# Two conditioned layers in one kernel: constants sent first, five betas on VectorE, two centrings on ScalarE, a bank for VectorE's scratch, new orders

## The reference

```python
h = _noise_encoding(t, E)                 # sin and cos of 5000 t * freqs, E = 128
h = jax.nn.silu(h @ W1 + b1)              # 512 wide
h = h @ W2 + b2
scale = (h @ Wsc + bsc)[:, None, :]
shift = (h @ Wsh + bsh)[:, None, :]
out = jax.nn.silu(scale * _layer_norm(x, gamma, beta) + shift)
out = out @ W_in + b_in
out = jax.nn.silu(scale * _layer_norm(out, gamma, beta) + shift)
out = out @ W_out + b_out
return out + x
```

## Time and profile before

| | us |
|---|---|
| median of 3 runs (82.25 to 82.94) | 82.47 |
| span of the profiled execution, first to last instruction | 80.7 |
| median less span | 1.77 |
| TensorE, matmuls busy | 75.0 |
| VectorE busy | 61.3 |
| ScalarE busy | 55.8 |
| GpSimd busy | 53.3 |

### The profile page before, as it was taken

One profiled execution on the slowest core, in us unless ns is written; L12 is line 12 of the kernel. 1 busy time (PEld: TensorE's weight loads), 2 busy tenths in 40 slices (PEclk: granted clock), 3 DMA queues, 4 the chain that ended last, 5 costly groups with the idle time before them and its releaser, 6 DMA issues.

```text
span 80.7 us, 1314 instructions
## 1 busy us (share of the span) xinstructions
PE 75.0 (93%) x293; PEld 37.2 (46%) x293; DVE 61.3 (76%) x181; ACT 55.8 (69%) x174; POOL 53.3 (66%) x63
## 2 busy tenths in 40 slices
PE   4999899999989999999999899999999899999950
PEld 1367547468633444444453443444454344445420
DVE  1085797879899979999879868886194697989560
ACT  4202410999939998977999997799936998967000
POOL 4000283999999999999999999999999303020000
PEclk9999999999999999999999999999999999999999
DMA  1799999999500000201130033030307200030835
GB/s 8 279 446 398 426 384 400 406 410 404 238 8 4 0 0 0 103 27 64 70 127 3 0 130 132 6 134 0 130 4 282 108 0 0 0 129 1 325 141 184
DMA packets 4903, 11.92 MB, mean 148 GB/s; under 512 B 672, under 2 KB 928, under 8 KB 4768
## 3 DMA queue, kind: packets, MB, share of 16 engines
q1 hardware_dynamic: 4752, 11.33, 36.7%
q10 hardware_dynamic: 144, 0.52, 1.6%
HBM read 7.65 MB, written 4.19 MB: 147 GB/s over the span
## 4 chain that ended last, share of the span: by engine, by line
POOL 41%; PE 27%; issue 25%; DVE 2%; POOLq 0%; ACT 0%; ACTq 0%
POOL act L326 16%; POOL act L331 11%; PE acc L978 11%; POOL act L320 7%; PE acc L849 6%; POOL rstd L304 5%; PE acc L954 5%; PE acc L989 2%; POOL rstd L314 1%; PE acc L852 1%; PE acc L999 1%; DVE o_sb L716 1%; PE stat_m L1007 1%; PE stat L898 0%; DVE spread L621 0%
## 5 line engine op out<-in xcount | busy, mean ns | idle before, releaser
L426 ACT ACTIVATE act<-act,cond 128x256 f32<-128x256 f32 x64 | 35.9, 594 | 5.6 <-POOL act L331 3.6
L978 PE MATMUL acc<-act,wout_sb 128*128 128x512 f32 x60 | 27.5, 600 | 0.0
L954 PE MATMUL acc<-act,win_sb 128*128 128x512 f32 x56 | 26.9, 608 | 0.5 <-ACT act L426 0.2
L331 POOL TENSOR_TENSOR act<-act,beta_sb 128x512 f32<-128x512 f32 x13 | 16.5, 1281 | 0.7
L326 POOL TENSOR_TENSOR act<-act,gamma_sb 128x512 f32<-128x512 f32 x13 | 16.6, 1284 | 0.3
L978 PEld LDWEIGHTS acc<-act,wout_sb 128*128 128x128 f32 x60 | 10.9, 189 | 12.4 <-issue 9.0
L446 ACT ACTIVATE squares<-acc,shift 128x256 bf16<-128x256 f32 x32 | 14.7, 464 | 2.1 <-PE acc L954 1.3
L704 DVE SCALAR_TENSOR_TENSOR act<-acc,shift,gamma_sb 128x256 f32<-128x256 f32 x32 | 14.3, 476 | 1.4 <-ACT squares L446 1.3
L954 PEld LDWEIGHTS acc<-act,win_sb 128*128 128x128 f32 x56 | 9.8, 190 | 10.5 <-issue 7.5
L711 DVE SCALAR_TENSOR_TENSOR act<-act,rstd,beta_ps 128x512 f32<-128x512 f32 x16 | 11.6, 742 | 3.4 <-issue 2.5
L716 DVE SCALAR_TENSOR_TENSOR o_sb<-acc,const_sb,x_sb 128x512 f32<-128x512 f32 (+1 forms) x17 | 11.9, 713 | 2.4 <-PE acc L978 2.3
(11 more groups left out here) (74 smaller groups left out, 53.7 us busy)
## 6 DMA issues: line engine op xcount, KB each, us to landing
out_dram<-o_sb SPq DMA_DIRECT2D x15, 256.0 KB, 2.0
x_sb<-x_dram SPq DMA_DIRECT2D x7, 512.0 KB, 12.8
w_sb<-w_dram SPq DMA_DIRECT2D x1, 1024.0 KB, 6.2
wss_sb<-wss_dram SPq DMA_DIRECT2D x1, 768.0 KB, 8.5
x_sb<-x_dram ACTq DMA_DIRECT2D x1, 512.0 KB, 3.9
w_sb<-w_dram SPq DMA_DIRECT2D x1, 256.0 KB, 4.1
gamma_sb<-gamma_dram SPq DMA_DIRECT2D x1, 256.0 KB, 6.4
wss_sb<-wss_dram SPq DMA_DIRECT2D x1, 256.0 KB, 8.7
```

What stands on the lines that cost most here:

```text
L331: nc.gpsimd.tensor_tensor(act1[:, p, :, b], act1[:, p, :, b], beta_sb[:], ALU.add).then_inc(z1_pool, 1)
L426: return nc.scalar.activation(buf[:, c, b], buf[:, c, b], ACT.Silu, bias=cond[:, 1, c, i:i + 1], scale=cond[:, 0, c, i:i + 1], **kw)
L954: mm = nc.tensor.matmul(y_slot(p, c)[:].rearrange("p b s -> p (b s)"), win_sb[:, k, c * P:(c + 1) * P], act1[:, p, k].rearrange("p b s -> ...
L978: mm = nc.tensor.matmul(bank_of(("O", p, c, 0, BP))[:].rearrange("p b s -> p (b s)"), wout_sb[:, k, c * P:(c + 1) * P], act2[:, p, k].rear ...
```

## The change

It has six parts. Line numbers in this section's rows are those of each file.

1. x[0] is issued by SyncE behind const, no longer by ScalarE; x[1] is loaded in two halves; x[2] stands ahead of W_in; the last three are x[6], x[7], x[5]. x is stored by item and then half, so that an item's 512 columns lie together.
2. `add_beta` on VectorE takes over GpSimd's `weigh_beta` for (2,1), (4,1), (4,0), (5,0) and (7,1).
3. `centre1` on ScalarE takes over GpSimd's `centre1` for (4,1) and (5,0); their rstd is multiplied in by `add_beta`.
4. All inputs of a statistics matmul stand in one tile, `stat_in`, one row for each matmul (`STATS`), and all powers in `POWERS`; VectorE's scratch moves to the bank `stat_m`; the mean of b_in uses a column of `beta_ps`.
5. `encoding` computes the turns from the constants, no longer from its first result. Products with zeros: 15 instead of 29 and 6 halves.
6. All orders are new. TensorE has 20 statistics matmuls, 16 of them behind the first product (before 15).

```diff
             sp.dma_start(const_sb[:], consts).then_inc(const_in, 16)
+            sp.dma_start(x_sb[:, 0], x[0]).then_inc(x_in[0, 0], 16)
...
-            act.dma_start(x_sb[:, 0], x[0]).then_inc(x_in[0], 16)
             nc.scalar.preload_act_table_set("silu_and_others")
...
-        x_sb = sb("x_sb", [P, NP, C, BP, S])
+        x_sb = sb("x_sb", [P, NP, BP, C, S])
...
+SHIFTED_DVE = ((2, 1), (4, 1), (4, 0), (5, 0), (7, 1))
+CENTRED_ACT = ((4, 1), (5, 0))
...
+            def add_beta(p, b):
+                dve.wait_ge(beta_ps_ready, 1)
+                dve.wait_ge(scaled_pool, count(SCALED_POOL, (p, b)))
+                if (p, b) in CENTRED_ACT:
+                    await_rstd(dve, "1", p)
+                    nc.vector.scalar_tensor_tensor(act1[:, p, :, b], act1[:, p, :, b], rstd_of("1", p, b), beta_ps[:],
+                                                   ALU.mult, ALU.add).then_inc(z1_shifted, 1)
+                else:
+                    nc.vector.tensor_tensor(act1[:, p, :, b], act1[:, p, :, b], beta_ps[:], ALU.add).then_inc(z1_shifted, 1)
...
+            def centre1(p, b):
+                i = BP * p + b
+                act.wait_ge(negm1_ready, count(NEGATED, GROUP_OF[p]))
+                nc.scalar.activation(act1[:, p, :, b], x_sb[:, p, b], ACT.Identity, bias=neg_m1[:, i:i + 1]).then_inc(centred_act, 1)
...
+            def dev_ps(n):
+                return stat_m[:, DEV_COL + 4 * n:DEV_COL + 4 * n + width(n)]
...
+            def stat_bank_free(i):
+
+                for kind, n in STATS[i - 1] if i else ():
+                    if kind == "mean1":
+                        pe.wait_ge(negm1_ready, count(NEGATED, n))
+                        if not summed_by_act(n):
+                            pe.wait_ge(dev_ready, count(DEVIATIONS, n))
...
             pe.wait_ge(zeros_set, 1)
-            warm(N_WARM)
+            warm(5)
```

More of the change, by code:

```diff
@@ L93 @@
 LEASED = ACCUMULATORS - 1
+SUMMED_BY_DVE = tuple(p for p in range(NP) if p not in SUMMED_BY_ACT)
+STAT_OF = {column: i for i, columns in enumerate(STATS) for column in columns}
+POWER_OF = {member: i for i, members in enumerate(POWERS) for member in members}
 def count(order, *items):
@@ L258, in bank_of, with await_x @@
+        def await_x(engine, p, b=None):
+            for i in range(BP) if p in BY_BATCH and b is None else (b,) if p in BY_BATCH else (0,):
+                engine.wait_ge(x_in[p, i], 16)
         def bank_of(product):
@@ L740, in _ @@
-            weigh_rowsums(0)
+            bn_stats1(1, 0)
+            bn_stats1(1, 1)
+            aggregate1(1, 1)
+            aggregate1(1, 0)
+            add_b2()
+            deviation(1)
+            weigh_gamma(0, 0, 0, 1)
+            weigh_gamma(0, 0, 1, 1)
+            negate_mean(1)
+            spread1(1, 1)
+            spread1(1, 0)
+            weigh_gamma(1, 0, 0, 2)
+            weigh_beta(0, 0, 1, 1)
+            weigh_beta(0, 0, 0, 1)
+            add_b_cond()
+            stats1_variance(1)
@@ L743, in _ @@
             mean_shift2(0)
-            stats1(4)
-            stats1_deviation(3)
-            weigh_gamma(2, 0)
+            bn_stats1(4, 0)
+            weigh_beta(2, 0, 0, 2)
+            weigh_rowsum0(1)
+            deviation(3)
+            negate_mean(3)
+            weigh_rowsum1(1)
+            spread1(3, 0)
+            weight2(0, 0, 0)
+            spread1(3, 1)
+            weight2(0, 0, 1)
+            mean_shift2(1)
+            add_beta(2, 1)
             stats1_variance(3)
-            weigh_rowsums(1)
+            bn_stats1(5, 1)
@@ L781, in _ @@
-            finish(1, 0)
-            normalise2(2, 0)
-            weigh_rowsums(4)
-            normalise2(2, 1)
+            aggregate1(7, 0)
+            weight2(2, 0, 1)
+            bn_stats1(7, 1)
+            weigh_rowsum0(3)
+            aggregate1(6, 0)
+            weigh_rowsum1(3)
+            add_beta(4, 1)
+            aggregate1(7, 1)
+            bn_stats1(6, 1)
+            aggregate1(6, 1)
+            mean_shift2(3)
+            variance2(2)
+            weight2(2, 1, 0)
+            weight2(2, 1, 1)
@@ L785, in _ @@
+            negate_mean(5)
+            add_beta(4, 0)
+            deviation(5)
+            finish(0, 1, 0, 2)
+            copy_deviation(5)
+            add_beta(5, 0)
+            square_deviation(5)
+            weigh_rowsum0(4)
+            weigh_rowsum1(4)
+            spread1_pairs(5)
+            finish(1, 0, 0, 2)
             weight2(3, 0, 0)
-            weight2(3, 1, 1)
-            stats1_deviation(5)
-            weight2(3, 1, 0)
             weight2(3, 0, 1)
             mean_shift2(4)
+            stats1_variance(5)
@@ L815, in _ @@
+            weight2(5, 1, 0)
+            finish(2, 1, 0, 2)
+            normalise2(4, 0)
+            weight2(5, 0, 0)
+            weight2(5, 1, 1)
+            weight2(5, 0, 1)
+            weigh_rowsum0(6)
+            weigh_rowsum1(6)
+            add_beta(7, 1)
+            finish(3, 1, 0, 2)
+            normalise2(4, 1)
+            variance2(5)
+            finish(3, 0, 0, 2)
             mean_shift2(6)
-            variance2(5)
-            finish(4, 0)
+            weigh_rowsum0(7)
@@ L830, in _ @@
+            weight2(7, 0, 1)
             weight2(7, 0, 0)
[L831 removed]
             variance2(7)
[L833 removed]
+            finish(4, 1, 0, 2)
+            normalise2(7, 1)
+            finish(4, 0, 0, 2)
+            normalise2(6, 1)
+            finish(5, 0, 0, 2)
+            finish(7, 1, 1, 1)
             normalise2(7, 0)
[L835 to L838 removed]
+            finish(5, 1, 0, 2)
```

927 lines of the change are left out of this document (452 added, 475 removed), and 15 rows, old and new, of tables (PRODUCTS, STATS).

## The result

The changed kernel is slower. Its median is 83.72 us, the kernel before took 82.36 beside it: ratio 1.013, 95% interval 1.007 to 1.020. Measured again it was 84.76 against 82.36, ratio 1.032 (1.023 to 1.040). Its own times spread from 82.7 to 85.8 over the two measurements, those of the kernel before from 82.0 to 82.9; the spread belongs to the change, as the experiments show. Seven of its eight executions took longer than any of the kernel before; the eighth took 82.73. Forecast were 81.9, with 80.8 to 83.4 as range: the 83.72 lie outside, on the side that had a chance of 0.17. The profiled execution took 83.94 us with a span of 82.1, before 80.7.

A forecast was written before the change was run, and what follows sets the result against it. It took the chain of waits as mostly GpSimd's (41%), then TensorE's (27%). Start 15.05 + products 55.0 + statistics 16 x 0.22 + waits 3.7 = 77.25 against 77.85, minus 0.6, giving 81.9 us; range 80.8 to 83.4.

The forecast's parts named there:

- The bytes ahead of beta are the same, so beta lands at 13.0.: Loads at the start: beta's landing stays at 4.39 + 8.6 = 13.0 us, as before.
- The two more issues on SyncE's queue: Start: issues for x[0] and x[1]'s halves, some 0.45 us each, hidden; with an idle queue they would cost 0.9.
- A slow clock: Rival, slower: fewer warming products leave the first layer products at 1.2 GHz, plus 1.3 us, 83.2; chance 0.09.
- From 13.0 to the first Silu: Start: after beta, 0.25 to see it, betas and add_b_cond to 14.3, Silu 0.60; first product's input at 14.95.
- the 1.0 us at the start: Start: the first product begins at 15.05 instead of 16.05 us, minus 1.0.
- x[3] late: Rival, slower: VectorE waits for x[3] at bn_stats of (3,1), from 16.6 us, becoming the bound; 82.9 or 83.6; chance 0.15.
- VectorE takes five betas, GpSimd loses them: VectorE pays 0.66 us per beta, covered by idle time and the earlier start; GpSimd's last beta ends at 58.0, not 62.5.
- ScalarE's centrings: ScalarE centres (4,1) and (5,0) between 30 and 38 us: 0.60 each, 1.2 in all, hidden in 1.4 idle.
- TensorE's waits: Between first and last product, waits at statistics and at products waiting for ScalarE total 3.7 us, against 3.5 before.
- waits go: Rival, faster: VectorE's small instructions cost 0.1 us less in the separate bank, about 1 us of waits goes, 80.9; chance 0.14.

The follow-up runs named there:

- f_gamma_act: Changed kernel with the old products with zeros (29 and 6 halves) and gamma issued by ScalarE at the start, x[0] staying on SyncE's queue: 81.57 us, ratio 0.994.
- b_few_warm: Kernel before with only the changed kernel's products with zeros (15, no halves): 84.65 us.
- a_same: The changed kernel measured again without an edit: 84.76 us, ratio 1.032 to the kernel before.
- e_start: Changed kernel with x[0] from ScalarE's queue, the old products with zeros but fewer at two places, and another VectorE order at the start: 81.53 us, ratio 0.991.
- a_warm: Changed kernel with the products with zeros as before, 29 and 6 halves instead of 15: 83.51 us.
- c_x0_act_warm: Changed kernel with two parts undone, x[0] from ScalarE's queue and the old products with zeros: 81.61 us, ratio 0.9925.
- d_bank_back: Changed kernel with x[0] from ScalarE's queue, the old products with zeros, and VectorE's scratch back in the statistics' bank: 82.29 us, ratio 1.003.

## Why the prediction was wrong, step by step

*The bytes ahead of beta are the same, so beta lands at 13.0.* This step failed. It took the bytes ahead for the only thing that sets a landing, and the trace of before couldn't show otherwise, as it had two queues in use. All in one queue cost W2 1.5 to 2.5 us and beta 1.9 to 2.5 us in every run. Alone, in the kernel before, it cost 1.7 us of time. The two more issues on SyncE's queue, taken as hidden, were not themselves the loss: f_gamma_act has x[1] in halves and x[0] there.

*A slow clock.* The rival was right in kind and misplaced. I priced it in the layers' products and held it unlikely since the gaps left were under 1 us. The layers' products all ran at 2.4 GHz. What ran at 1.2 GHz was the condition's work, ahead of them and on the path: 0.85 at W2's product, 0.65 at those of Wsc and Wsh. The reason I gave fails as well, and not only because the loads were late: in b_few_warm, with the loads in time, TensorE's longest gap behind its first zeros was 0.80 us, and W2's product took 1.94 all the same. Alone it moved the first product by 1.25. The rule that I cited, that the low level is the default and activity lifts it (the Trainium skill, "TensorE: Matmul & The Clock Gate", Part 1: The HAM clock gate), agrees with a_same's fall to 0.50, a row that the trace of before did not have.

The two causes hide behind each other. With either one undone the first product still came at 17.1 or 18.3, and only both together brought 16.3.

*From 13.0 to the first Silu.* Failed by 1.2 even with both causes gone. I counted from beta and let VectorE be free at 13.0; it was free at 14.39. e_start shows that the 1.0 us at the start then would have bought 0.1 to 0.5 at the end, because VectorE is busy almost without a gap from 12.5 to 23 and x[3] comes at 17.6.

*x[3] late.* Not in the changed kernel itself, whose x[3] landed at 18.69 and was wanted at 20.13. In a_warm and e_start it held VectorE at the named place. The last section has what went with it.

*VectorE takes five betas, GpSimd loses them.* Right. `add_beta` took 0.68 without a scale and 0.74 with one (forecast 0.66 with 0.60 to 0.74); ScalarE's centrings took 0.71 each (forecast 0.60), hidden. GpSimd's last beta ended at 59.6 with a start 3.7 us later than forecast, and at 57.1 in c_x0_act_warm (forecast 58.0). Its wait at the end of the earlier trace rows is gone.

*TensorE's waits.* Forecast 3.7, measured 1.8: the outcome of the rival "waits go" and more, but not by its mechanism. That rival let VectorE's small instructions take 0.1 less in a bank into which TensorE doesn't write. The two spreads of pair 1, first in c_x0_act_warm with that bank, then in d_bank_back with the shared one, take the same:

```profile
13.47 0.34 DVE L687 SCALAR_TENSOR_TENSOR stat_in<-stat_m,stat_in 128x1 f32<-128x1 f32 x2
```

```profile
14.23 0.34 DVE L687 SCALAR_TENSOR_TENSOR stat_in<-stat,stat_in 128x1 f32<-128x1 f32 x2
```

Of 17 idle times of its weight loads over 0.4 us between the first and the last product of the kernel before 9 are left. Seven of them stand at statistics, among them these two:

```profile
44.14 0.30 PEld L1019 LDWEIGHTS stat<-stat_in,share_w 128*128 128x128 f32 x2 [0.82 <-issue]
...
62.98 0.30 PEld L1019 LDWEIGHTS stat<-stat_in,share_w 128*128 128x128 f32 x2 [0.63 <-issue]
```

The other two stand at products, 0.65 behind VectorE's `finish` and 0.68 that the profile puts down to issue. My walk put 3.0 at nine statistics, and 0.7 more at products that wait for ScalarE; none that the profile puts down to ScalarE was over 0.4. Of the gain, d_bank_back gives some 0.35 to the bank; the rest lies with the betas and the orders made for them, which no run told apart.

So the sum was wrong by 3.7 at the start and by 1.9, the other way, in the waits. Had the start gone as c_x0_act_warm has it, the forecast of 81.9 would have stood next to 81.6, but by luck: a start forecast 1.2 too early and waits forecast 1.9 too long would have hidden each other.

## What to carry to other kernels

A move of the first loads into one queue is a change of its own, to be priced by a run, also where the bytes ahead of a load stay the same. Products that keep TensorE warm belong to whatever small products stand on the path to the first real one, so count those before taking them out. And an earlier start is worth what the engine that is full next lets through: look behind the start for that engine before booking the gain.
